# Slot stage of a decoder kernel: TensorE does the h-side z product ahead of the spread of the root in each beat

## What is computed

```python
for _ in range(NUM_ITERS):                       # 3
    sn = rmsnorm(slots, slot_norm_w)
    q_proj = sn @ Wq.T
    scores = jnp.einsum('bkd,bmd->bkm', q_proj, k_proj) * SCALE
    attn = jax.nn.softmax(scores, axis=-2)       # over the slots k
    attn = attn / (jnp.sum(attn, axis=-1, keepdims=True) + EPS)
    updates = jnp.einsum('bkm,bmd->bkd', attn, v_proj)
    slots = gru_cell(updates, slots, ...)        # r, z and n gates
```

## Time and profile before

| | us |
|---|---|
| median of 3 runs | 1553.99 (1552.95 to 1559.47) |
| profiled execution, time | 1554.87 |
| profiled execution, span of its instructions | 1553.0 |
| PE busy in the span | 1385.3 (89%) |
| PE busy from 1000 to 1100 us, in the slot stage | 98.46 of 100 |

### The profile page before, as it was taken

How to read it: one execution, slowest core, us unless ns; L and a number is a source line. 1 busy time by engine, 2 the same in 40 slices (tenths; PEclk the granted TensorE clock), 3 DMA queues, 4 the chain that set the end, 5 groups by cost and what they waited for, 6 DMA issues and landing times. The chain is left out here.

```text
span 1553.0 us, 27695 instructions
## 1 busy us (share of the span) xinstructions
PE 1385.3 (89%) x8898; PEld 1081.1 (70%) x8898; DVE 1215.6 (78%) x2143; ACT 1105.3 (71%) x2296; POOL 1223.9 (79%) x845
## 2 busy tenths in 40 slices
PE   5899999999999999999987799999999999549993
PEld 2676667667766766666665588878888777449993
DVE  1899999999999999999998177777777787735452
ACT  3888998889888988898885466666666655215552
POOL 1899999999999999999998344567777776635665
PEclk8899999999999999999999599999999999769997
DMA  4334342343334333433231344323427000047771
GB/s 137 97 103 138 123 130 94 129 125 132 115 118 131 112 123 109 145 119 122 97 123 57 113 169 151 131 66 121 145 89 298 13 8 10 23 141 195 212 210 32
DMA packets 114560, 182.75 MB, mean 118 GB/s; under 512 B 12210, under 2 KB 75637, under 8 KB 114432
## 3 DMA queue, kind: packets, MB, share of 16 engines
q1 hardware_dynamic: 109888, 172.68, 34.5%
q0 software_dynamic: 4544, 8.47, 1.6%
HBM read 126.37 MB, written 55.66 MB: 117 GB/s over the span
## 5 line engine op out<-in xcount | busy, mean ns | idle before, releaser
L423 POOL TENSOR_TENSOR hc<-state,c_rows 128x1024 f32<-128x1024 f32 x256 | 599.7, 2375 | 26.4 <-DVE state L721 26.3
L721 DVE TENSOR_TENSOR_SCAN state<-ps_op,inp 128x512 f32<-128x512 f32 x352 | 406.8, 1205 | 7.8 <-issue 3.3
L902 PE MATMUL ps_y<-ident,hc 128*128 128x128 f32 x2048 | 255.5, 274 | 22.2 <-POOL hc L423 21.7
L902 PEld LDWEIGHTS ps_y<-ident,hc 128*128 128x128 f32 x2048 | 228.4, 142 | 64.0 <-POOL hc L423 47.4
L550 ACT ACTIVATE ps_op<-dt,a_neg 128x512 f32<-128x512 f32 x352 | 238.4, 690 | 40.5 <-DVE state L721 36.1
L721 DVE TENSOR_TENSOR_SCAN state<-da_side,ps_op 128x512 f32<-128x512 f32 x160 | 184.0, 1199 | 16.6 <-PE ps_op L919 16.6
L704 DVE TENSOR_TENSOR inp<-dtx,ps_b 128x1024 f32<-128x1024 f32 x128 | 153.7, 1200 | 45.7 <-POOL dtx L396 25.7
L1348 POOL TENSOR_TENSOR rs<-ms,m_half 128x4 f32<-128x4 f32 x48 | 68.0, 1417 | 121.7 <-DVE ms L1569 121.5
L1486 ACT ACTIVATE ex<-sc,nmx,ctx_r 77x128 f32<-77x128 f32 x192 | 92.4, 482 | 97.9 <-DVE nmx L1582 97.9
L557 ACT ACTIVATE inpT<-dtxT,b_tok 128x256 f32<-128x256 f32 x320 | 135.8, 500 | 0.0
L408 POOL TENSOR_TENSOR inp<-dtx,b_rows 128x1024 f32<-128x1024 f32 x48 | 120.2, 2504 | 0.0
(11 more groups left out here) (251 smaller groups left out, 3156.8 us busy)
## 6 DMA issues: line engine op xcount, KB each, us to landing
c_rows<-bc_rows SPq DMA_DIRECT2D x128, 512.0 KB, 3.7
sorted_x<-pad_rows SPq DMA_DIRECT2D x8, 4160.0 KB
w<-in_L_ffn_W SPq DMA_DIRECT2D x78, 256.0 KB
b_rows<-bc_rows SPq DMA_DIRECT2D x48, 256.0 KB, 5.1
vw<-vw_rows SPq DMA_DIRECT2D x16, 462.0 KB
vw_rows<-vw_out SPq DMA_DIRECT2D x16, 384.0 KB
xrow<-sorted_x SPq DMA_DIRECT2D x39, 130.0 KB
x_tok<-in_x SPq DMA_DIRECT2D x16, 256.0 KB, 4.6
```

What stands on the lines that cost most here:

```text
L423: pool.tensor_tensor(hc[:, n % RING], state[:, n % RING], over_c(c_rows[:, slot, n % 2]), ALU.mult).then_inc(hc_ready, 1)
L721: dve.tensor_tensor_scan(state[:, n % RING, c], decays, inputs, 0.0, ALU.mult, ALU.add).then_inc(state_ready, 1)
L902: ins = pe.matmul(ps_y[:, b, c], hc[:, n % RING, c, b * P:(b + 1) * P], ident[:], start=False, stop=n == NS - 1, is_transpose=True, skip_g ...
```

## The change

PE's order in each beat is altered in one place. The h-side z product (one 128x512 product, in two passes) stands ahead of `root_spread` and no longer behind it. It changes beats 2 to 47, those in which both are there. Nothing is added or removed, and no other engine's order changes.

```diff
             if live(n - 1):
                 den(n - 1)
+            if live(n - 2):
+                gate_h(n - 2, 1, ps_z, z_read)
             if live(n):
                 root_spread(n)
-            if live(n - 2):
-                gate_h(n - 2, 1, ps_z, z_read)
             if live(n - 1):
                 den_spread(n - 1)
```

## The result

The kernel became slower: 1572.4 us median of 4 runs (1570.34 to 1574.53), against 1555.88 (1552.95 to 1559.47, 4 runs) before. (Three of these four runs were known ahead of the prediction, with a median of 1553.99.) The ratio is 1.01, with a 95% interval of 1.0078 to 1.0122. The profiled execution took 1571.23 us, its span 1569.4; that is 16.4 more than before on both.

What follows compares the result with a forecast made beforehand. A circle between DVE and PE without DVE slack was taken to bound the later beats. Ten groups at 1.15 (11.5), plus 0.6, 0.5, 1.3, less 0.2, made 13.7; from 1554.87 to 1568.6, forecast 1568, range 1560 to 1576.

Steps and rivals of the forecast that it cites:

- the likeliest case: The forecast's own case for the whole kernel: slower, at 1564 to 1573 us, chance 0.68.
- The circle: DVE `ms`, PE r product, `den`, spread, DVE `sc`, DVE's queue without slack to the next `ms`; a later spread delays it equally.
- faster: If DVE had slack between `sc` and `ms`, only PE's 4.6 us of waits for POOL would change: 1549, chance 0.06.
- Plain beats, +0.8 each: Beats 17, 20 to 47 (11): `ms` already stops the r product and comes 0.83 later with the count beat's spread.
- Early beats, nothing: Beats 2 to 14 except 12: `ms` starts 0.44 behind `gate_hn`, so the r product still hides it; no cost.
- the cover: Early beats' room to hide a later `ms`, called all but used up: a further 0.1 us would show.
- Row beats, +0.1 to +0.3: Beats 18, 21 to 42 (9): 0.42 gained from POOL's wait, but `make_u` waits for `sc`, starting at 5.73 against 5.63.
- Count beats, +0.15: Beats 16, 19 to 46 (11): `ms` 0.39 later makes the r product 0.25 later, partly counted in the row beat.
- Three beats, 28.33 + 1.15: The circle closed over three beats: 0.25 to the count beat's r product, 0.83 to the plain `ms`, up to 0.11 late load.
- Beats 45 to 47, +1.3: End of the stage: 0.5 for count beat 46 and 0.8 for plain beat 47.
- Beat 44, at -0.2: `pre` waits 1.31 for PE, so DVE slack takes 0.8 off, but that beat's row products wait 0.6.
- The rule weighed: Row beats: POOL's `rs` meeting DVE's `h` loses up to 2 us more; collision rival 1573 to 1577, chance 0.14.

Runs made afterwards that it cites:

- z_count: Against the kernel before, the h-side z product ahead of the spread in the 11 count beats alone; 1568.65 us, ratio 1.0088.
- ms_early: The kernel before with DVE's `mean_sq` moved ahead of `new_in` and `normaliser` in row and count beats; 1544.5 us, ratio 0.9915.
- z_plain: Against the kernel before, the h-side z product ahead of the spread in the 23 plain beats alone; 1561.22 us, ratio 1.0038; run again 1563.45 us.
- z_row: Against the kernel before, the h-side z product ahead of the spread in the 12 row beats alone; 1561.27 us, ratio 1.0035.
- spread_first: The kernel before with, in count beats, the spread ahead of `den` on PE and `sc` ahead of `rdn` on DVE; 1552.44 us, ratio 0.9976.
- the two ms_early kernels with z first: The changed kernel with `mean_sq` moved early on DVE, 1561.8 us; the same with row products also behind the x-side z products, 1553.73 us.

## Why the prediction was right

The forecast was 1568, and the measured 1572.4 lies in its range; the likeliest case was the one that came. It lies 0.6 under the upper end of that case, and two of the four runs lie above it, so this side of the edge is in part luck. Of the 4.4 us by which the forecast was too low, 1.9 is the fourth run of the kernel before, which moved its median, and the rest is the sum: against its 13.7 the profiled pair shows 16.6 in the beats, and 16.4 in all.

- **The circle** was read rightly. That DVE has no slack from `sc` to `ms` decided the sign. z_count shows it by itself: 11 later spreads, ahead of plain beats, make those typically 0.86 longer, though the order on PE in the plain beats is the old one. ms_early shows it from the other side. The rival "faster" is refuted: the row "PE for `rs`" did vanish, and the time grew.
- **Plain beats, +0.8 each:** typically +0.91. Of this, 0.87 is the later r product, and two terms are mis-sized. The first is "I take 0.83" for the spread, which ends 0.90 later. In the early plain beat the z product starts at 926.63 and the spread at 927.57, 0.94 behind it, where 0.86 was taken from the earlier trace rows. There the z product stands behind four transposes; ahead of the spread it stands behind `den`.
- **The order on PE itself** was put at nothing ("PE's own work is unchanged"), and it costs 0.04 a beat. From the start of `den` to the x-side z products the plain beat 23 takes 2.63 after and 2.59 before; z_count has the 0.04 in its count beats and not in its plain ones. In 46 beats this is 1.8 us, an estimate.
- **Early beats, nothing:** right for the circle. They are 8.75 long, not 8.71, which makes 0.80 for beats 2 to 11 (a quarter us of it in beat 2), 0.17 for 13 and 14, but their r product stays at 0.86 to 0.87 behind `gate_hn` from beat 3 to 15: this is the order on PE and not the cover. "A further 0.1 us on it would show" was wrong by the prediction's own figures. With 0.21 from `ms` to the r product and 0.86 to the r product without a wait, an `ms` is hidden up to 0.65 behind `gate_hn`. It stood at 0.46, and at 0.64 in beat 14, and did not show.
- **Row beats, +0.1 to +0.3:** this is the largest miss; most took +0.45. The step that failed is "`sc` is over at 1.45 behind" the spread, taken as the start of the row products. `make_u` started 1.65 behind it (1068.45 to 1070.10). Its first weight load comes 0.23 after `sc` has ended (1069.84), where I had taken 0.06 between the two. The spread itself started 4.36 behind `gate_hn` and not 4.28, and the late load, named as "up to 0.11", cost 0.07 more. Beat 12 was predicted at 0.6 and took 0.73.
- **Count beats, +0.15:** about right, +0.1 each on average up to beat 40, then -0.28 in beat 43 and +0.42 in beat 46.
- **Three beats, 28.33 + 1.15:** 29.73, +1.40, just above the 29.4 to 29.5 named: +0.45 up to the count beat's r product (0.25 forecast), +0.91 from there to the plain beat's `ms` (0.83 forecast), and 0.04 behind it. Beats 15 to 44 hold 14.31, where the forecast's terms for them make 11.8.
- **Beats 45 to 47, +1.3:** +0.59, since beat 45 took 0.73 less than before. Beat 44, at -0.2, was wrong: it took +1.32. (44 is a row beat and 45 a plain one; the list of plain beats ahead of the prediction has 44 for 45.)
- **"The beats behind have no spread, what follows shifts as a whole":** beat 48 took 0.80 more. PE in beat 48 after, and then before:

```profile
1335.80 1.02 PE L1883 MATMUL ps_hn<-h,whhT 128*128 128x512 f32 x2
...
1340.06 0.41 PE L1838 MATMUL ps_u<-hot,not_after 128*128 128x32 f32 x2 [1.49 <-ACT tok L1512]
```

```profile
1320.09 1.02 PE L1883 MATMUL ps_hn<-h,whhT 128*128 128x512 f32 x2
...
1323.56 0.41 PE L1838 MATMUL ps_u<-hot,not_after 128*128 128x32 f32 x2 [0.70 <-issue]
```

The count of the last group waits for ACT to read the row products (`tok`). In ACT's queue that read stands behind `nn`, which needs DVE's queue, which the last spread had made late: at 4.26 behind `gate_hn` instead of 3.47. The lateness outlived the last spread by a beat. The experiments bear this out. z_plain, in which the spread of beat 47 is late, has the count at 4.26 as well. z_count and z_row, in which it is not, have it at 3.47; in z_row, whose beat 48 opens at 1325.42:

```profile
1328.89 0.41 PE L1838 MATMUL ps_u<-hot,not_after 128*128 128x32 f32 x2 [0.69 <-issue]
```

**The rule weighed** was the collision of POOL's root with DVE's `h` in the row beat. They did meet: `h` ran from 1066.82 to 1067.55. POOL in time:

```profile
1066.78 1.05 POOL L1348 TENSOR_TENSOR rs<-ms,m_half 128x4 f32<-128x4 f32 x1
...
1085.84 2.02 POOL L1348 TENSOR_TENSOR rs<-ms,m_half 128x4 f32<-128x4 f32 x1 [2.86 <-DVE ms L1569]
```

The root of the row beat started 0.04 ahead of `h` and took 1.05 as before (1.06); in the plain beat, started behind `keep`, it took 2.02. So the 2 us of that rival were not paid, and the excess over the sum came from `make_u`, the spread and the order on PE. The Trainium skill, SBUF — State Buffer, section "Who interferes with whom", states that the order of issue decides which of the two waits. The root's two lengths agree with that. The other half, as the prediction has it, that the one that issues second is blocked until the first is done, does not fit here: `h`, issued second, took 0.73 (0.69 before) and was over at 1067.55, while the root, by the profile's times for POOL, ran to 1067.83.

## What to carry to other kernels

An engine that is busy 98% of the time may still be the one that waits. Follow one signal round over all engines, and ask of each later product how much slack the next instruction on that round has. A wait shows up where the slack ran out, one or two beats behind its cause; only moving the edit from one kind of beat to another tells the two apart. And when the round is tight, look on it for a small instruction that only reads, as the 0.15 us `ms` here, and put it ahead of the long ones: that was worth 0.85% here, with `den` and the spread left where they were.

## What was unexpected of the hardware

- **The granted clock fell in single beats.** In beat 18 of z_plain it was 0.86, twice, to within 0.01 us of length; after it was 1.00 there, with nearly the same work. In beat 48 it was 1.00 before and after, but 0.67 and 0.74 in the two executions of z_plain. Before and after are in fact the exceptions: the other eleven profiled executions all had 0.67 to 0.85 in beat 48, which took them 10.74 to 14.61 us (9.26 before). Beat 48 of z_plain in time:

```profile
1327.67 0.41 PE L1838 MATMUL ps_u<-hot,not_after 128*128 128x32 f32 x2 [1.48 <-ACT tok L1512]
...
1330.09 2.06 PE L1887 MATMUL ps_z<-h,whhT 128*128 128x512 f32 x2
```

PE had been idle for 1.48 us, and the z product behind it took 2.06, twice its 1.02 elsewhere: the lower level, 1.2 GHz. After had the same idle time (1.49) ahead of the same instruction, and its z product took 1.10; z_row had only 0.69 there (0.70 before) and still fell to 0.84. So the idle time alone does not decide it. Such a fall costs 1.5 to 4.5 us in a stretch of 10, as much as a term of the sum. What starts it stays open, and so does how often beat 48 has it in the unprofiled runs behind each median. The small ratios above, of z_plain, z_row, spread_first and the two ms_early kernels with z first, may hold some of it; their beats 2 to 47 are the firmer figures.
- **The z product takes 0.94 behind `den` and 0.86 behind transposes**, from its start to the start of what follows, here four transposes both times: 926.63 to 927.57 after, and 927.43 to 928.29 before. Beat 48 of the kernel before, where z already stood behind `den`, has 0.94 too (1325.14 to 1326.08). Behind `den` it is shown as 1.10 long, not 1.02.
- **The gap from a DVE result to PE differed**: 0.21 from the start of `ms` (0.15 long) to the r product, so 0.06 from its end, against 0.23 from the end of `sc` to the weight load of the row products and 0.26 to their first product.
